# A mixture-of-experts stage: sorted rows that carry weight and gate, and results added into the output by indirect DMAs

## The reference

```python
gate = xf @ Wg + bg                      # 8192 x 8 experts
topv, topi = jax.lax.top_k(gate, 2)      # two experts per token
probs = softmax(topv)
comb = zeros.at[token, topi].set(probs)
h = relu(einsum('nc,ecf->nef', xf, W1) + b1)   # 128 -> 512, 8 experts
y = einsum('nef,efc->nec', h, W2) + b2         # 512 -> 128
out = einsum('nec,ne->nc', y, comb)
x = x + gb * out                         # gb: one row of 128 per batch
```

## Time and profile before

| | before |
|---|---|
| median of 3 runs | 2460.11 us (2452.89 to 2465.32) |
| the profiled execution | 2452.23 us, span 2450.5 us |
| TensorE busy | 1804.4 us, 74% |
| VectorE busy | 1372.6 us, 56% |
| ScalarE busy | 1194.4 us, 49% |
| GpSimd busy | 902.1 us, 37% |
| HBM read, written | 38.84 MB, 59.90 MB |
| mean granted TensorE clock | 0.863 |

### The profile page before, as it was taken

One profiled execution on the slowest core, in us unless ns is written; L12 is line 12 of the kernel. 1 busy time (PEld: TensorE's weight loads), 2 busy tenths in 40 slices (PEclk: granted clock), 3 DMA queues, 4 the chain that ended last, 5 costly groups with the idle time before them and its releaser, 6 DMA issues.

```text
span 2450.5 us, 46984 instructions
## 1 busy us (share of the span) xinstructions
PE 1804.4 (74%) x14634; PEld 974.3 (40%) x14634; DVE 1372.6 (56%) x3660; ACT 1194.4 (49%) x1780; POOL 902.1 (37%) x1806
## 2 busy tenths in 40 slices
PE   3878888898658887799999999997322057777750
PEld 2734444444443333344444444444321035444430
DVE  5456555555577777656666666664323024444448
ACT  1356667766547876334444444444312135445430
POOL 1233333333132333434444444443466733344330
PEclk9999999999759999589999999998555578888875
DMA  4194000000100000000000000001011211111125
GB/s 134 39 386 181 0 0 0 0 0 0 44 9 1 0 0 24 11 1 1 0 0 0 0 0 0 0 0 70 22 38 37 67 53 53 55 58 56 52 79 161
DMA packets 71967, 99.91 MB, mean 41 GB/s; under 512 B 9346, under 2 KB 43010, under 8 KB 70852
## 3 DMA queue, kind: packets, MB, share of 16 engines
q1 hardware_dynamic: 42736, 42.11, 5.7%
q10 hardware_dynamic: 20052, 37.77, 4.3%
q0 software_dynamic: 9088, 18.89, 2.3%
HBM read 38.84 MB, written 59.90 MB: 40 GB/s over the span
## 4 chain that ended last, share of the span: by engine, by line
PE 23%; issue 13%; POOL 12%; DVE 6%; ACT 2%; DVEq 2%; POOLq 1%; DMA 1%; SPq 0%; ACTq 0%
PE OP L1667 6%; POOL y_dram L413 6%; POOL h_dram L402 5%; PE M L1626 4%; PE M L1582 2%; PE M L1596 2%; DVE mx L1051 2%; PE SP L1647 2%; PE M L1622 2%; PE M L1617 1%; ACT shared L649 1%; PE OP L1696 1%; PE SP L1898 1%; POOLq L254 1%; DVE st L1010 1%
## 5 line engine op out<-in xcount | busy, mean ns | idle before, releaser
L668 ACT ACTIVATE pt<-SP 128x1024 f32<-128x1024 f32 (+1 forms) x512 | 459.7, 921 | 364.9 <-PE SP L1647 364.8
L1667 PE MATMUL OP<-pt,vs 128*32 128x256 f32 (+1 forms) x4096 | 434.5, 362 | 15.3 <-ACT pt L668 13.8
L1051 DVE TENSOR_REDUCE mx<-M 128x2 f32<-128x512 f32 (+1 forms) x384 | 257.2, 690 | 118.9 <-PE M L1626 115.8
L1667 PEld LDWEIGHTS OP<-pt,vs 128*32 128x32 f32 x4096 | 176.9, 110 | 182.3 <-issue 51.0
L413 POOL DMA_INDIRECT y_dram<-oT,dest x156 | 156.6, 1004 | 245.7 <-DVE oT L1310 209.6
L760 ACT ACTIVATE pt<-SP,b 128x512 f16<-128x512 f32 x156 | 107.2, 687 | 243.7 <-PE SP L1947 242.2
L1947 PE MATMUL SP<-ksT,shared 128*128 128x512 f16 x468 | 153.3, 462 | 90.2 <-DVE ksT L1286 90.2
L482 POOL TENSOR_SCALAR_AFFINE_SELECT pt<-pt 128x256 f32<-128x256 f32 x512 | 196.0, 407 | 0.0
L1647 PE MATMUL SP<-shared,ksT 32*128 32x256 f16 (+1 forms) x2048 | 172.3, 262 | 2.3 <-ACT ksT L641 1.2
L479 POOL TENSOR_TENSOR spare<-ones 128x1 f32<-128x1 f32 x256 | 49.4, 193 | 310.0 <-ACT pt L668 309.9
L1626 PE MATMUL M<-ksT,shared 24*128 24x128 f16 (+1 forms) x1024 | 154.5, 251 | 0.0
(11 more groups left out here) (269 smaller groups left out, 3426.1 us busy)
## 6 DMA issues: line engine op xcount, KB each, us to landing
h_dram<-logit ACTq DMA_DIRECT2D x1, 35904.0 KB, 101.0
st<-h_dram SPq DMA_DIRECT2D x39, 264.0 KB, 2.7
rows<-g_dram SPq DMA_DIRECT2D x4, 2048.0 KB, 7.2
pt<-y_dram SPq DMA_DIRECT2D x64, 128.0 KB, 2.4
x_sb<-in_x SPq DMA_DIRECT2D x8, 512.0 KB, 8.9
pt<-in_w SPq DMA_DIRECT2D x4, 1024.0 KB, 7.2
out<-x_sb SPq DMA_DIRECT2D x32, 128.0 KB, 1.9
y_dram<-oT,dest POOLq DMA_INDIRECT x156, 2.3
```

The costliest lines, as they stand in the source:

```text
L668: act.activation(pt[:, u % 4, :, 0:W], SP[u % 2][:, :, 0:W], ACT.Exp, scale=SCALE).then_inc(s["exp"], 1)
L1051: dve.tensor_reduce(to, M[:, k % 2, :].rearrange("p (j k) -> p j k", j=2 if k < 8 else 4), AX.X, ALU.max).then_inc(s["mred"], 1)
L1667: last = pe.matmul(OP[32 * g:32 * g + 32, j // 2, c + q0:c + T], vs[:, par, k, HG * j + g, :], pt[:, u % 4, i, k * T:k * T + T - q0], star ...
```

## The change

- A row in `h_dram` now has 260 full-precision fields (1040 bytes): 128 that hold the high and low half-precision parts, the 128 values of the token's gate row, and four numbers: token, weight of the second choice, difference of the weights, and expert of the first choice. `hrow` has two buffers of a quarter each instead of room for all 64 tiles; a quarter's rows are written once the sends of two quarters before have landed. ScalarE has a second copy per batch, of the gate row.
- The low part is computed by VectorE in its loop (`keep_low` is gone), the weights are converted in ScalarE's iterations b = 2 to 5, and GpSimd does `weight_low` first and then the four `send`s.
- SP stores x to the output in four DMAs in the sorting stage.
- Blocks have four buffers for rows, results, `dest` and `gain`. `targets` copies the token numbers and computes the weight `gain`, and waits for the scatters of block g - 4. `leave` is four operations that multiply the result by `gain` and by the gate row.
- `spread_y` scatters into the output with `compute_op` add, and waits before each block until all scatters so far have landed, because a token's two copies lie in different blocks. Empty rows go to 512 extra rows behind the output.
- The combination is gone, with `y_dram` and `c12`.
- `blank` is 4160 bytes per partition, so the fill of `h_dram` moves 72 MB instead of 36.

The diff, cut to its core:

```diff
-FLD = 264
+RW = 2 * D + 4
...
-        hTr = sb("hT", [P, NT * FLD // 2])
+        hTr = sb("hT", [P, 2 * QN * RW])
...
+        xg = hTr[:, 0:16 * RW].rearrange("p (k n c) -> p k n c", k=4, c=RW)
+        ys = hTr[:, 16 * RW:16 * RW + 16 * D].rearrange("p (k n d) -> p k n d", k=4, d=D)
...
+                    if n == 3:
+                        od = out[0:B * T, :].rearrange("(n p) d -> p n d", p=P)
+                        for i in range(4):
+                            sp.dma_start(od[:, QN * i:QN * (i + 1), :], x_sb[:, QN * i:QN * (i + 1), :]).then_inc(y_out, 16)
...
-                if g >= 2:
-                    sp.wait_ge(k["xT"], g - 1)
-                    sp.wait_ge(k["dst"], g - 1)
-                sp.dma_start(xg[:, g % 2].rearrange("p r w -> p (r w)"),
+                if g >= 4:
+                    sp.wait_ge(k["yE"], g - 3)
+                sp.dma_start(xg[:, g % 4].rearrange("p n c -> p (n c)"),
...
             def spread_y():
 
                 k = blk_s
+                pool.wait_ge(y_out, 16 * 4)
                 for g in range(NBLK):
                     pool.wait_ge(k["yE"], g + 1)
-                    pool.wait_ge(k["dst"], g + 1)
+                    if g:
+                        pool.wait_ge(k["out"], 16 * 4 * g)
                     for r in range(4):
                         pool.indirect_dma_start(
-                            out=y_dram, out_offset=bass.IndirectOffsetOnAxis(ap=dest[:, g % 2, r:r + 1], axis=0),
-                            in_=ys[:, g % 2, r, :], in_offset=None).then_inc(k[f"out{g % 2}"], 16)
+                            out=out, out_offset=bass.IndirectOffsetOnAxis(ap=dest[:, g % 4, r:r + 1], axis=0),
+                            in_=ys[:, g % 4, r, :], in_offset=None, compute_op=ALU.add).then_inc(k["out"], 16)
...
-            keep_low()
             weight_low(3)
-            send(NQ - 1)
+            for q in range(NQ):
+                send(q)
...
+                        if q >= 2 and at % QB == 0:
+                            act.wait_ge(r[f"rows{q % 2}"], 16 * 2 * QN * (q // 2))
...
+                        act.activation(place[:, :, D:2 * D], rows[:, at:at + 1, :].to_broadcast([P, TT, D]),
                                        ACT.Copy).then_inc(r["bkE"], 1)
...
-                for c in range(CHUNKS):
-                    weight_high(3, c)
+                    if b == 2:
+                        act.wait_ge(r["blanked"], 32)
+                    if 2 <= b < 2 + CHUNKS:
+                        weight_high(3, b - 2)
...
+                    if 1 <= b <= B:
+                        par = (b - 1) % 2
+                        dve.wait_ge(s["h"], b)
+                        if b >= 3:
+                            dve.wait_ge(r["bk"], b - 2)
+                        dve.tensor_tensor(hh[:, par, 1, :], hcur[:, par, :], hh[:, par, 0, :], ALU.subtract).then_inc(r["lo"], 1)
...
                 def targets(g):
 
-                    if g >= 2:
-                        dve.wait_ge(k[f"out{g % 2}"], 64 * (g // 2))
...
+                    token, c2, dc, first = [xg[:, g % 4, :, 2 * D + c] for c in range(4)]
+                    dve.wait_ge(k[f"in{g % 4}"], 16 * (g // 4 + 1))
+                    if g >= 4:
+                        dve.wait_ge(k["out"], 16 * 4 * (g - 3))
+                    dve.tensor_copy(dest[:, g % 4], token)
+                    dve.scalar_tensor_tensor(gain[:, g % 4], first, bexp[:, g:g + 1], dc, ALU.is_equal, ALU.mult)
                     dve.drain()
...
+                    dve.tensor_tensor(gain[:, g % 4], gain[:, g % 4], c2, ALU.add)
...
                     dve.wait_ge(k["y"], g + 1)
-                    dve.tensor_scalar(ys[:, g % 2].rearrange("p r d -> p (r d)"), bank[4 + g % 2], 1.0 / WSCALE, None,
-                                      ALU.mult).then_inc(k["yE"], 1)
+                    for r in range(4):
+                        last = dve.scalar_tensor_tensor(ys[:, g % 4, r, :], bank[4 + g % 2][:, r * D:(r + 1) * D],
+                                                        gain[:, g % 4, r:r + 1], xg[:, g % 4, r, D:2 * D], ALU.mult, ALU.mult)
+                    last.then_inc(k["yE"], 1)
...
-                for b in range(B):
-                    dve.wait_ge(k[f"yin{b % 8}"], 32 * (b // 8 + 1))
...
```

More of the change, by code:

```diff
@@ L73, in program @@
         x_sb = sb("x_sb", [P, NT, D])
-        hTr = sb("hT", [P, NT * FLD // 2])
+        hTr = sb("hT", [P, 2 * QN * RW])
         hT = hTr[:, 0:NT * P]
-        hrow = hTr[:].bitcast(F16).rearrange("p (n c) -> p n c", c=FLD)
+        hrow = hTr[:].rearrange("p (k n c) -> p k n c", k=2, c=RW)
         rows = sb("rows", [P, B, D])
@@ L245, in program @@
         exp_s = [sems("exp", 0, "c cT cE hid relu lo row rowE y term acc turn done")]
-        rt_s = sems("route", 0, "lo bk bkE sel pos m2 ex slot count counts table blank blanked rows")
-        blk_s = sems("blk", 0, "xT xE hid relu lo y yE dst in0 in1 out0 out1 comb done yin0 yin1 yin2 yin3 yin4 yin5 yin6 yin7")
+        rt_s = sems("route", 0, "lo bk bkE sel pos m2 ex slot count counts table blank blanked rows0 rows1")
+        blk_s = sems("blk", 0, "xT xE hid relu lo y yE dst in0 in1 in2 in3 out")
         block = ctx.enter_context(nc.Block())
@@ L379, in _ @@
             pool.memset(vs[:, :, :, :, DH:DH + 1], 1.0)
-            def keep_low():
-                s, r = norm_s[3], rt_s
-                for b in range(B):
-                    pool.wait_ge(s["h"], b + 1)
-                    if b >= 2:
-                        pool.wait_ge(r["bk"], b - 1)
-                    pool.tensor_tensor(hh[:, b % 2, 1, :], hcur[:, b % 2, :], hh[:, b % 2, 0, :],
-                                       ALU.subtract).then_inc(r["lo"], 1)
-                    if b % QB == QB - 1 and b > QB:
-                        send(b // QB - 1)
             def send(q):
@@ L1229, in place @@
                 dve.drain()
-                dve.tensor_reduce(rm[:, 0:QN], rt1, AX.X, ALU.add)
-                dve.drain()
-                dve.tensor_copy(hrow[:, at, 2 * D + 2:2 * D + 3], rm[:, 0:QN])
-                dve.drain().then_inc(r["slot"], 1)
+                if q >= 2:
+                    dve.wait_ge(r[f"rows{q % 2}"], 16 * 2 * QN * (q // 2))
+                fields = hrow[:, q % 2, :, 2 * D:2 * D + 4]
+                dve.tensor_reduce(fields[:, :, 3:4], rt1, AX.X, ALU.add)
+                dve.tensor_copy(fields[:, :, 0:1], toki[:, at].unsqueeze(2))
                 dve.wait_ge(r["ex"], q + 1)
-                c1, c2 = c12[:, at, 0:1], c12[:, at, 1:2]
                 dve.tensor_scalar(rm[:, 0:QN], second[:], 1.0, None, ALU.add)
                 dve.drain()
-                dve.reciprocal(c1, rm[:, 0:QN])
+                dve.reciprocal(rm[:, 0:QN], rm[:, 0:QN])
                 dve.drain()
-                dve.tensor_tensor(c2, c1, second[:], ALU.mult)
+                dve.tensor_scalar(cpair[:, :, 0:1], rm[:, 0:QN], 1.0 / WSCALE, None, ALU.mult)
+                dve.scalar_tensor_tensor(cpair[:, :, 1:2], rm[:, 0:QN], 1.0 / WSCALE, second[:], ALU.mult, ALU.mult)
+                dve.drain()
+                dve.tensor_copy(fields[:, :, 1:2], cpair[:, :, 1:2])
+                dve.tensor_tensor(fields[:, :, 2:3], cpair[:, :, 0:1], cpair[:, :, 1:2], ALU.subtract)
+                dve.drain().then_inc(r["slot"], 1)
             def table():
```

117 lines of the change are left out of this document (35 added, 82 removed).

## The result

The change made the kernel slower: 2535.4 us median (2532.41 to 2538.84, 4 runs) against 2457.5 (2452.89 to 2465.32, 4 runs), ratio 1.031, 95% interval 1.028 to 1.035. The forecast was 2345 us. The profiled execution took 2537.34 us, span 2535.5.

A forecast was written before the change was run, and what follows sets the result against it. Limits: VectorE's plain tail in the combination, GpSimd's single order in sorting, mostly TensorE's loop in the blocks. 2450.5 - 73.3 - 57 + 2 + 11 + 4.4 = 2337.6 us span; forecast 2345 us, range 2288 to 2400.

The forecast's parts named there:

- The blank fill: Fill of h_dram, 36 to 72 MB: ends near 320 us into the span, costs nothing; uncovered 101 us.
- Sorting stage: Subtraction to VectorE, weights' conversion earlier (13.5 us); sends run through, first block load at 1919.2 instead of 1976.15: -57 us.
- Rival (d): Sorting stage: sends don't close up, likely 15 to 30 us come back, 2360 to 2375 us; chance 0.06 for 15 or more.
- Combination: Tail after the blocks: its 73.8 us go, some 0.5 us remain after the last landing, -73.3 us.
- Rows of 1040 bytes: Sends in the sorting stage, rows from 528 to 1040 bytes: 0 to 3 us, taken 0.5.
- Block stage, start: First loads of the blocks grow from 264 to 520 KB: +2 us, once.
- The loop: Block stage: TensorE's gap grows from 2.07 to 2.50 us, period from 10.0 to 10.3 us, +11 us.
- rival (c): Block stage: the clock stays up, blocks run at 8.8 to 9.0 us, 52 us less, 2293 us; chance 0.09.
- The adding scatter: Block stage: an addition lands in 3.6 us, GpSimd's loop of 7.7 us stays hidden under 10.3.
- (a): Block stage: additions set the pace, from a landing of 6.2 us; example 2401 us; chance without (b) 0.11.
- (b): Block stage: additions make it slower than before, period 13.3, landing 9.2 us; 2503 us at 10 us; chance 0.06.
- Tail: From the 38th leave to the last landing: 16.7 us instead of 12.3, +4.4 us.

The follow-up runs named there:

- e1: Kernel after with ScalarE's two fill DMAs exchanged, the 256 KB one first and the 72 MB one second: 2386.6 us, ratio to before 0.970.
- e13: e1 with 16 tiny GpSimd operations after every 8 sends and the weights' conversion moved behind the first quarter: 2345.2 us.
- e17: e1 with 1 tiny GpSimd operation after every 8 sends: 2346.2 us.
- e4: e1 with sends of 528 instead of 1040 bytes a row, into a tensor of their own: 2388.1 us.
- e9: e1 with GpSimd waiting for landing after every 8 sends, and take of the next block ahead of leave and the third low: 2370.1 us.
- e11: e9 with the blocks' results written instead of added: 2290.3 us.
- e16: e13 with 4 instead of 16 tiny GpSimd operations after every 8 sends: 2338.4 us, ratio to before 0.953.
- e10: e1 with GpSimd waiting for the landing after every 16 sends: 2358.5 us.
- e7: e1 with the blocks' results written instead of added: 2380.0 us.
- e2: Kernel before with a second DMA of 264 KB behind its 36 MB fill on ScalarE's queue: 2525.9 us, ratio 1.027.
- e6: e1 with a small GpSimd operation and a drain between two sends: 2613.4 us.

## Why the prediction was wrong

**The blank fill** failed, and with it the forecast: "202 us end near 320 us into the span, 1400 before anyone asks: nothing". That holds for the data (e1: 158.04 us busy in 189). What I left out is that the edit issues two DMAs, and who stands behind the second: ScalarE itself, with the whole attention. In before the fill was the last DMA on that queue, and its issue costs 0.43 us. Price: 153 us by the trace, 148.8 by e1.

The spans add up as follows; each term is after minus forecast:

| term | forecast | after | difference |
|---|---|---|---|
| start of the sorting stage | 1696.8 | 1854.65 | +157.9 |
| to the first send | 55.2 | 57.4 | +2.2 |
| first to last send | 163.2 | 197.8 | +34.6 |
| to the first load | 4.0 | 5.5 | +1.5 |
| to the first `leave` | 20.1 | 18.2 | -1.9 |
| 37 periods | 381.2 | 378.4 | -2.8 |
| from the 38th `leave` | 17.2 | 23.6 | +6.4 |
| span | 2337.6 | 2535.5 | +197.9 |

Of the first row 153 us are ScalarE's; the rest lies in the stages between, which no edit touched.

**Sorting stage.** The front was right: 13.5 us for the weights (e13 gets 15 back), first send within 2.2 us. So were the four stores of x at nothing: GpSimd's first addition waits for VectorE. Wrong was "the sends run through". It rested on a quarter needing 27.7 us, read from iterations with no sends beside them. Beside an unbroken row of sends an iteration takes up to 21 us. Rival (d) named this ("the sends slow beside a busy VectorE") and priced it at 15 to 30 us; it was 34.6 in after, 41 in e1. e17, with 162.5 us, shows that the 163 were there to be had.

**Combination** went as forecast: nothing but the landing stands behind the last scatter. **Rows of 1040 bytes**: no cost that can be told (e4 against e1, 0.6 us in the span). **Block stage, start**: 18.2 us instead of 18.06 before; the +2 was none.

**The loop.** Right: gap 2.51 for 2.50, period 10.23 for 10.3, clock 0.84 (2140 to 2240 us), so rival (c) is out. Beside it stood the Trainium skill, page "TensorE: Matmul & The Clock Gate", section "Why this matters for your kernels", which warns only of longer pauses, and by which the clock would have stayed up; with pauses of 2.51 us it did not. **The adding scatter**: "hidden" was right, its size wrong. The landing of 3.6 us was right (e9: median 3.6). The prediction also drew on the Trainium skill, page "DMA: Bandwidth & Descriptors", section "Two DMAs through the same engine are not ordered", by which an addition would land hardly later than a plain write. Counted from the end of the issue that is nearly so: the next block waits 2.5 us in e9 and 2.05 in e11. Counted from its start the addition is over about 1 us later, since the issue itself is longer. That is the step that failed here, the issue taken as unchanged: 1.55 us instead of 0.96, issues 1.86 us apart and not 1.33. The loop is 9.6 us at least and 10.27 in the mean (e9), not 7.7, so the margin was not 2.6 us but about none. In 14 blocks of after the DMA was last. Rivals (a) and (b) did not occur, but after stands on the edge of (a): e9, with TensorE's gap opened, gained nothing. That the loop stayed hidden was therefore in part luck.

**Tail**: +6.4 us, again the issues: two blocks of four 1.86 us apart, and GpSimd was a block behind when the last `leave` came.

The sign was missed by one term. With the fill mended (e1) the change is worth 3.0%. With the rows of sends mended too (e17, one run) the time is 2346.2 us and the sends take 162.5, where the forecast had 2345 and 163. Moving the conversion as well, which the forecast did not have, gives 4.7% (e16, 2338.4 us).

**What stays open** is through what a row of sends reaches the other engines. It isn't width, landing or time. In e10 (first pause after the 16th send, at 1777.6) the iterations beside the 7th to 11th send still took 2.66 us and `choose` behind them 6.7. In after, e1, e4 and e7, with the same order of work up to there, the second of these iterations took 4.9 to 7.2 us, and `choose` in e1 25.7 us. That fits something that depends on what follows on GpSimd's queue; no run here looks into it.

## What to carry to other kernels

Price a DMA by what stands behind it on the queue of the engine that issues it: a small one behind a large one holds a compute engine for nearly the large one's time, so issue the small one first, and the large one last. Where a step is said to be hidden beside other work, take its duration from a row where that other work runs. When two loops through the same block are within a few per cent of each other, shortening one buys nothing.

## What the runs showed of the hardware

- The issue of a second DMA on ScalarE's queue took 171.61 us behind 72 MB (186.5 us to land) and 86.56 us behind 36 MB (96.8 us in e2); that of a first one, or of a large one behind a small one, 0.43 to 0.65 us.
- While GpSimd issues indirect DMAs in an unbroken row, a VectorE step of 0.5 us grows to 2.80 us (after) and iterations of 2.66 us over three engines to 5, 13 and 21 us (e1). One memset of 0.12 us after every 8 prevents it (e17).
- An indirect DMA with addition takes 1.55 us of GpSimd's time, a plain one 0.96. The following wait for its landing is 2.5 us instead of 2.05 (medians, e9 and e11).
- A small operation of 0.30 us and a drain on GpSimd between two indirect DMAs put them 3.4 us apart instead of 1.27 (e6).
